# The extra turn in the middle of an expert stream, and three blocks' records written earlier

## The chip, the cores and the metric

The kernel runs on one core of a Trainium2 chip. The metric is the device time of one execution in microseconds (us). The median of three runs of the kernel before is 436.33 us (435.52 to 436.38).

## What is computed

One layer of a graph network, then a mixture of experts, over 1024 nodes with 512 features in float32:

```python
x = x + relu(segment_sum(edge_weight[:, None] * (layernorm(x) @ W)[src], dst) + bias)   # 16384 edges
xt = layernorm(x)
scores = sigmoid(xt @ Wg.T + bg);  w, idx = top_k(scores, 2);  w = w / w.sum(-1)        # 64 experts
nx = standardised rows of xt
h1 = nx @ (gamma[e][:, None] * W1[e]) + ...;  h3 = the same with W3                      # 512 x 256 per expert
y = sum over the two chosen experts e of w[e] * ((silu(h1) * h3) @ W2[e] + b2[e])
x = x + y + (a small shared expert on every row)
```

The reference computes every expert for every row and weights most of them with zero. The kernel only computes the two that a row has chosen. The weights of all 64 experts are read once: 1.5 MB for each expert.

## The kernel before

**First stage (to about 165 us).** The edges are turned into a dense matrix of 1024 x 1024 sums, and the graph layer is eight blocks of 128 rows. For each block s GpSimd computes the deviations of the second norm (`deviations(s)`, L540 to L550), ScalarE writes the standardised rows, SP stores them in DRAM as `nx_rows`, TensorE and VectorE route them, and GpSimd prepares the list (`values`, L558) and the shared expert's rows (`stacked`, L561 to L572). Every engine works in its own order, which is written out by hand, and waits on semaphores for the others.

**Lists.** For every expert there is a list of records (token, destination) in DRAM, `slots`. Records of blocks 0 to 4 (`DRAM_BLOCKS` = 5) are written there with two indirect scatters of 128 records of 8 bytes each (`scatter_records`, L533) while the stage runs. Then SP loads the first 64 places of each list (L380, semaphore `list_in`), and TensorE adds the records of blocks 5 to 7 to it on the chip. DRAM gets these three blocks' records too, since experts with over 64 tokens continue there, and only the overflow uses them. In the kernel before this is done after the first four gathers.

**The stream (from about 170 us).** There are 33 turns. A turn j takes a pair of experts: up to 64 tokens of each are gathered from `nx_rows` by GpSimd (L588), turned by TensorE (L1464), scaled by VectorE, multiplied with W1 and W3 (`up`, L1476), turned (L1498), put through SiLU on ScalarE (L734) and multiplied by the other half on VectorE (L1133). They are then multiplied with W2 (`down`, L1506), copied out by ScalarE (L741) and scattered by GpSimd to `totals` in DRAM (L592). One turn is the extra one: it takes one chunk of up to 128 tokens of an expert whose list has overflowed, with this one expert's weights alone (`over_up` L1483, `over_down` L1490, `over_silu` L748, `over_product` L1143). `EX` is its number, 31, and `LAST` is 32, so that it stands before the last pair. Which expert it is, is known from a small table early in the stream. Its list is loaded by SP in turn 4 (L387, after all records are written) and converted by VectorE (`over_index`) in turn 16.

**Weights.** Six slots hold a turn's weights (`SLOTS` = 6). SP issues the two up loads (1 MB each, L346) of turn j + 6 when turn j's up product is done (`h_ps`), and the down load (1 MB, L349) of turn j + 5 when turn j - 1's down product is done (`y_ps`). For the extra turn they are 0.5 MB each (L392, L396). All go through SP's queue in this order.

**The end.** When all scatters have landed, SP loads `totals` back in eight loads (L436). The last pair isn't scattered: TensorE puts its rows in place with eight matmuls (L1601), ScalarE and VectorE add up, and SP stores eight blocks.

Of the kernel before, what the change touches and what calls it, by code (L numbers as in the profile page):

```python
# [11 lines left out]
NB = N // P  # L12
# [21 lines left out]
PAIRS = EXPERTS // 2  # L34
OVER = 2 * N // CAP
# [3 lines left out]
SLOTS = RING // 2 + 2  # L39
XG, AHEAD = 4, 4  # L40
YS = 4
NOWHERE = 60000.0
EX, LAST = PAIRS - 1, PAIRS
BY_DVE = 1
XS = EX % YS


def pair_of(j):
    return j if j < EX else PAIRS - 1

# [1 line left out]
def moe_gnn(nc, x, src, dst, ew, W, bias, Wg, bg, gamma, beta, W1, b1, W3, b3, W2, b2,  # L54
# [18 lines left out]
    with ctx:  # L73
# [240 lines left out]
        def _(sp):  # L314
# [87 lines left out]
            for j in range(LAST - SLOTS + 1):  # L402
                if j == AHEAD:
                    sp.wait_ge(tokens_ready, 1)
                    for i in range(2):
                        sp.wait_ge(rec_out[i], 32 * NB // 2)
                    load_over(0)
                sp.wait_ge(h_ps, j + 1)
                if j + SLOTS == LAST:
                    sp.wait_ge(y_ps, j)  # L410
                    load_over_down(0)
                if j + SLOTS == EX:
                    load_over_up(0)
                else:
                    load_up(pair_of(j + SLOTS), j % SLOTS)
                if 1 <= j < LAST - SLOTS:
                    sp.wait_ge(y_ps, j)
                    load_down(j + SLOTS - 1, (j - 1) % SLOTS)
            sp.wait_ge(y_ps, LAST - SLOTS + 1)
            load_down(pair_of(LAST), LAST % SLOTS)  # L420
            R2 = sp.value_load(rounds_sb[0:1, 1:2], min_val=1, max_val=OVER)
# [22 lines left out]
        def _(pool):  # L444
# [129 lines left out]
            for s in range(NB):  # L574
                deviations(s)
                if s > DRAM_BLOCKS:
                    values(s - 1)
                if s >= 1:
                    stacked(s - 1)
                if 1 <= s <= DRAM_BLOCKS:  # L580
                    scatter_records(s - 1)
            values(NB - 1)
            pool.wait_ge(at_ps, 2 * NB)
# [11 lines left out]
            pool.wait_ge(list_ready, 1)  # L595
            for j in range(AHEAD):
                gather(TOK[:, j:j + 1], j)
            stacked(NB - 1)
            pool.wait_ge(list_in, 16)
            for s in range(DRAM_BLOCKS, NB):  # L600
                scatter_records(s)
            pool.wait_ge(zero_out, 16)
            for j in range(LAST + 1):
                b = j + AHEAD
                if b <= LAST:
                    if b >= XG:
                        pool.wait_ge(xe_ps, b - XG + 1)
                    if b == EX:
                        pool.wait_ge(over_ready, 1)
                    gather(TOK[:, pair_of(b):pair_of(b) + 1] if b != EX else over_idx[:, 0:1], b % XG)  # L610
                if j == AHEAD:
                    pool.wait_ge(share_out, 16)
                    pool.wait_ge(share_at_ready, 1)
                    g.indirect_dma_start(wsh, None, shares, bass.IndirectOffsetOnAxis(ap=share_at, axis=0),
                                         bounds_check=2 * N - 1, oob_is_err=False).then_inc(wsh_in, 16)
                if j < LAST:
                    pool.wait_ge(y_ready, j + 1)
                    scatter(DST[:, j:j + 1] if j != EX else over_idx[:, 1:2], j % YS)
            pool.wait_ge(tokens_ready, 1)
            R2 = pool.value_load(rounds_sb[0:1, 1:2], min_val=1, max_val=OVER)  # L620
            with pool.If(R2 > 1):
# [11 lines left out]
        def _(act):  # L633
# [117 lines left out]
            for j in range(PAIRS + 1):  # L751
                if j >= 2:
                    act.wait_ge(hT_ps, j - 1)
                if j < LAST:
                    hidden(j, j % 2)
                if j:
                    if j - 1 >= YS:
                        act.wait_ge(y_out[(j - 1) % YS], 16 * ((j - 1) // YS))
                    result(j - 1, (j - 1) % 2, (j - 1) % YS)
                if j == LAST:  # L760
                    hidden(j, j % 2)
                if j >= 2:
                    act.wait_ge(hT_ready, j - 1)
                if j == EX:
                    act.wait_ge(tokens_ready, 1)
                    over_silu(j, j % 2, 0)
                    R2 = act.value_load(rounds_sb[0:1, 1:2], min_val=1, max_val=OVER)
                else:
                    silu(j, j % 2, lambda h: slice(2 * pair_of(j) + h, 2 * pair_of(j) + h + 1))
            act.wait_ge(y_out[LAST % YS], 16 * (LAST // YS))  # L770
            result(LAST, LAST % 2, LAST % YS)
            with act.If(R2 > 1):
# [16 lines left out]
        def _(dve):  # L789
# [367 lines left out]
            for j in range(PAIRS + 1):  # L1157
                if j == 0:
                    over_table()
                if j == 1:  # L1160
                    over_experts()
                    last_shares()
                if j + 1 <= LAST and j + 1 != EX:
                    if j >= 1:
                        dve.wait_ge(h_ps, j)
                    rows(j + 1, (j + 1) % 2)
                if j == 0:
                    for b in range(3, LATE):
                        add_shared(b)
                    dve.wait_ge(stack_ready, NB)  # L1170
                if j == 2:
                    stack_out(NB - 1, bank[5])
                if j in late_turn:
                    add_shared(LATE + late_turn.index(j))
                if j == PAIRS // 2:
                    over_index(0)
                if j + 1 == EX:
                    dve.wait_ge(tokens_ready, 1)
                    at = over_at_expert(0)
                    dve.wait_ge(h_ps, j)  # L1180
                    over_rows(j + 1, (j + 1) % 2, at)
                if j >= 2:
                    dve.wait_ge(y_ps, j - 1)
                if j == EX:
                    over_product(j, j % 2, at)
                    dve.wait_ge(wsh_in, 16)
                    link(v.tensor_copy(tokf, TOK[:, pair_of(LAST):pair_of(LAST) + 1]))
                    link(v.tensor_scalar(token_at, iota[:, 0:NB], -float(P), tokf, ALU.mult, ALU.add))
                    for i in range(NB):
                        ins = v.tensor_scalar(place_last[i], iota[:, :], token_at[:, i:i + 1], wsh, ALU.is_equal, ALU.mult)  # L1190
                    ins.then_inc(last_places, 1)
                else:
                    product(j, j % 2, lambda h: slice(2 * pair_of(j) + h, 2 * pair_of(j) + h + 1))
                if j == EX:
                    R2 = dve.value_load(rounds_sb[0:1, 1:2], min_val=1, max_val=OVER)
            with dve.If(R2 > 1):
                with dve.Fori(1, R2) as t:
# [28 lines left out]
        def _(pe):  # L1226
# [352 lines left out]
            with pe.If(R2 > 1):  # L1579
                with pe.Fori(1, R2) as r:  # L1580
# [2 lines left out]
                    hold(pe)  # L1583
                    turn_rows(0, 0)
                    pe.wait_ge(xe_ready, j + 1)
                    pe.wait_ge(w13_in[OS], r * 32 + (32 * (PAIRS // SLOTS) + 32))
                    hold(pe)
                    over_up(0)
                    turn_hidden(j, 0)
                    whole_bank(bank[0])  # L1590
                    pe.wait_ge(w2_in[OS], r * 16 + (16 * (PAIRS // SLOTS) + 16))
                    pe.wait_ge(y_ready, j)
                    hold(pe)
                    over_down(j, 0)
# [31 lines left out]
```

## Time and profile before

| | us |
|---|---|
| median of three runs | 436.33 |
| the profiled execution | 438.14 |
| its span | 436.4 |
| TensorE busy | 398.3 (91%) |
| VectorE busy | 212.7 (49%) |
| ScalarE busy | 156.8 (36%) |
| GpSimd busy | 172.7 (40%) |

The span is the time from the first to the last instruction of the profiled execution; its own time contains a little more around it. Busy times are sums over the whole span, and stages with different bounds are mixed in them. A wait is shown as the idle time before an instruction with what ended it. A transfer has two numbers: when its instruction was issued, and the time from there to its landing.

### The profile page before, as it was taken

The numbers are of one execution on the slowest core, as the hardware profiler recorded it, in microseconds if no ns is written. First come the engines' busy times: TensorE is split into PE (matmuls) and PEld (weight loads), VectorE is DVE, ScalarE is ACT, GpSimd is POOL, SyncE is SP. The second block draws the span as 40 slices with busy tenths as digits, with TensorE's granted clock in tenths as the row PEclk, the third lists the DMA queues.
The fourth block names the chain that finished last, engine by engine and source line by source line (L and its number), as shares of the span: only waits on it lengthen the run. The fifth ranks groups of instructions, "written<-read, shape, count | busy, mean of one in ns | idle before, by whom it ended". The sixth has DMA issues, their size and how long they took to land.

```text
span 436.4 us, 6405 instructions
## 1 busy us (share of the span) xinstructions
PE 398.3 (91%) x1898; PEld 208.4 (48%) x1899; DVE 212.7 (49%) x696; ACT 156.8 (36%) x387; POOL 172.7 (40%) x275
## 2 busy tenths in 40 slices
PE   6988999999999998999999999978978877988986
PEld 5556768655655556434344344433333333443431
DVE  8899998136566676542332332331223213112437
ACT  8777786223233220423233233321231231132232
POOL 2769996315655646632432232231122123111100
PEclk9999999999999998999999999998999999898999
DMA  7999970400004572789999999999999999999378
GB/s 239 222 341 410 404 273 32 141 25 26 24 24 159 207 293 74 199 324 407 403 407 407 408 403 409 407 407 408 408 403 408 408 406 405 405 401 379 152 258 324
DMA packets 44022, 129.15 MB, mean 296 GB/s; under 512 B 8054, under 2 KB 9270, under 8 KB 43858
## 3 DMA queue, kind: packets, MB, share of 16 engines
q1 hardware_dynamic: 38242, 120.45, 73.1%
q0 software_dynamic: 5744, 8.28, 5.3%
q8 instruction: 16, 0.26, 0.2%
q14 instruction: 20, 0.16, 0.1%
HBM read 119.64 MB, written 17.85 MB: 315 GB/s over the span
## 4 chain that ended last, share of the span: by engine, by line
PE 71%; issue 8%; POOL 6%; DMA 6%; DVE 5%; SPq 1%; ACT 1%; DVEq 0%; ACTq 0%; POOLq 0%
PE bank L1476 24%; PE bank L1339 13%; PE bank L1506 11%; PE bank L1498 4%; PE bank L1288 4%; PE bank L1464 3%; PE bank L1261 3%; DMA A<-nx_rows,A 2%; DMA w<-totals 2%; PE bank L1327 2%; PE bank L1360 1%; POOL slots L533 1%; POOL M L500 1%; POOL AT L500 1%; PE bank L1348 1%
## 5 line engine op out<-in xcount | busy, mean ns | idle before, releaser
L1133 DVE SCALAR_TENSOR_TENSOR osl<-bank,b13T,osl 128x64 f32<-128x64 f32 x128 | 27.5, 277 | 162.0 <-ACT osl L734 162.0
L1476 PE MATMUL bank<-w,xhT 128*64 128x512 f32 x352 | 85.7, 630 | 15.0 <-issue 14.3
L727 ACT COPY xh<-bank 128x512 f32<-128x512 f32 x33 | 19.3, 585 | 145.1 <-PE bank L1476 142.1
L1339 PE MATMUL bank<-HW,AT 128*128 128x512 f32 x128 | 58.2, 593 | 0.0
L1476 PEld LDWEIGHTS bank<-w,xhT 128*64 128x64 f32 x352 | 26.4, 143 | 59.0 <-issue 56.8
L592 POOL DMA_INDIRECT totals<-GW,A x16 | 16.0, 1003 | 89.5 <-PE bank L1464 70.5
L592 POOL DMA_INDIRECT totals<-osl,A x16 | 16.1, 1004 | 71.2 <-PE bank L1464 61.8
L1506 PE MATMUL bank<-w,osl 128*64 128x512 f32 x176 | 41.9, 594 | 0.5 <-DVE osl L1133 0.5
L588 POOL DMA_INDIRECT A<-nx_rows,A x33 | 34.1, 1032 | 12.3 <-issue 9.8
L1339 PEld LDWEIGHTS bank<-HW,AT 128*128 128x128 f32 x128 | 22.9, 191 | 21.0 <-issue 21.0
L643 ACT ACTIVATE osl<-iota,eT 128x128 f32<-128x128 f32 x90 | 27.8, 387 | 9.9 <-PE bank L1288 9.9
L734 ACT ACTIVATE osl<-bank,b13T 128x64 f32<-128x64 f32 x128 | 29.8, 314 | 3.8 <-PE bank L1498 0.9
L1498 PEld LDWEIGHTS bank<-ident,xh 128*128 128x128 f32 x132 | 18.3, 208 | 26.8 <-issue 25.1
L1261 PE MATMUL bank<-GW,xhT 128*128 128x512 f32 x64 | 29.3, 597 | 1.0 <-DMA GW<-in_L_gnn_W_dram 1.0
L500 POOL TENSOR_SCALAR AT<-iota,small 128x128 f32<-128x128 f32 x30 | 25.5, 861 | 1.5 <-POOL small L489 1.4
L1498 PE MATMUL bank<-ident,xh 128*128 128x128 f32 x132 | 24.6, 309 | 0.7 <-ACT xh L727 0.7
L1506 PEld LDWEIGHTS bank<-w,osl 128*64 128x64 f32 x176 | 13.3, 137 | 25.0 <-issue 24.8
L1464 PE MATMUL bank<-ident,A 128*128 128x128 f32 x132 | 21.6, 286 | 1.0 <-DMA A<-nx_rows,A 1.0
L1476 PE MATMUL bank<-HW,xhT 128*64 128x512 f32 x80 | 18.3, 597 | 4.3 <-issue 4.3
L1118 DVE TENSOR_TENSOR xhT<-xhT,bT 128x512 f32<-128x512 f32 x31 | 21.4, 692 | 1.1
L1117 DVE TENSOR_TENSOR xhT<-bank,gT 128x512 f32<-128x512 f32 x31 | 21.1, 680 | 0.3 <-PE bank L1464 0.3
L500 POOL TENSOR_SCALAR M<-iota,small 128x128 f32<-128x128 f32 x23 | 19.7, 865 | 2.4 <-POOL small L489 1.5
(238 smaller groups left out, 594.9 us busy)
## 6 DMA issues: line engine op xcount, KB each, us to landing
w<-in_L_ffn_W_dram SPq DMA_DIRECT2D x66, 1024.0 KB, 19.0
A<-in_L_ffn_W_dram SPq DMA_DIRECT2D x15, 1024.0 KB, 18.6
HW<-in_L_ffn_W_dram SPq DMA_DIRECT2D x10, 1024.0 KB, 19.2
AT<-in_L_ffn_W_dram SPq DMA_DIRECT2D x5, 1024.0 KB, 19.9
totals<-w SPq DMA_DIRECT2D x1, 4096.0 KB, 26.4
w<-totals SPq DMA_DIRECT2D x8, 512.0 KB, 7.5
out_dram<-X SPq DMA_DIRECT2D x8, 256.0 KB, 2.3
X<-in_x_dram SPq DMA_DIRECT2D x3, 512.0 KB, 8.6
```

The source lines that it names most:

```text
L500: ins = g.tensor_scalar(Mq[q % 4][:, k, :], iota[:, :], keyw[h % 2][:, 0, t:t + 1], keyw[h % 2][:, 1, t:t + 1], ALU.is_equal, ALU.mult)
L588: g.indirect_dma_start(xg[b], None, nx_rows, bass.IndirectOffsetOnAxis(ap=index, axis=0), bounds_check=N - 1, oob_is_err=False).then_inc(x ...
L592: g.indirect_dma_start(totals, bass.IndirectOffsetOnAxis(ap=index, axis=0), ysb[b], None, bounds_check=2 * N - 1, oob_is_err=False).then_i ...
L643: ins = a.activation(osl[:, h % 2, k, :], iota[:, :], ACT.Abs, bias=eT[:, 1, ds(j * 32 + 8 * h + k, 1)])
L734: ins = a.activation(sl[b][:, m, CAP * h:CAP * h + CAP], bank[4][:, m * P + CAP * h:m * P + CAP * h + CAP], ACT.Silu, bias=b13T[:, 0, m, c ...
L1133: ins = v.scalar_tensor_tensor(hT[b][:, m, CAP * h:CAP * h + CAP], bank[4][:, (HC + m) * P + CAP * h:(HC + m) * P + CAP * h + CAP], b13T[: ...
L1261: ins = t.matmul(bank[6 + u][:, :], xhT[:, u, c, :], GW[:, c, :], start=(c == 0), stop=(c == DC - 1))
L1339: ins = t.matmul(bank[4 + s % 2][:, :], AT[:, s % 2, k, :], HW[:, k, :], start=(k == 0), stop=(k == NB - 1))
L1464: ins = t.transpose(bank[b][:, c * P:(c + 1) * P], xg[i][:, c:c + DC * (P - 1) + 1:DC], ident[:, :])
L1476: ins = t.matmul(bank[2 + b][CAP * h:CAP * h + CAP, :], xe[b][:, c, CAP * h:CAP * h + CAP], up_w[v][:, h, :, c, :], start=(c == 0), stop=( ...
L1498: ins = t.transpose(bank[4][:, i * P:(i + 1) * P], hraw[b][:, at:at + HC * (P - 1) + 1:HC], ident[:, :])
L1506: ins = t.matmul(bank[6 + b][CAP * h:CAP * h + CAP, :], hT[b][:, m, CAP * h:CAP * h + CAP], down_w[v][:, h, m, :], start=(m == 0), stop=(m ...
```

## The change

Two things are changed. `EX` becomes 17, so that the extra turn stands in the middle, turns 18 to 32 take pairs 17 to 31, and all loads, lists and registers of the extra turn follow it. Its list is converted in turn 8. And each of the last three blocks' records are written in GpSimd's loop like those of the others. The first of them waits for the list's load (`list_in`) in this place, and block 7's are written after the first four gathers and before `stacked(7)`.

```diff
--- before.py
+++ after.py
@@ -40,13 +40,13 @@
 XG, AHEAD = 4, 4
 YS = 4
 NOWHERE = 60000.0
-EX, LAST = PAIRS - 1, PAIRS
+EX, LAST = PAIRS // 2 + 1, PAIRS
 BY_DVE = 1
 XS = EX % YS
 
 
 def pair_of(j):
-    return j if j < EX else PAIRS - 1
+    return j if j < EX else j - 1
 
 
 
@@ -406,16 +406,18 @@
                         sp.wait_ge(rec_out[i], 32 * NB // 2)
                     load_over(0)
                 sp.wait_ge(h_ps, j + 1)
-                if j + SLOTS == LAST:
-                    sp.wait_ge(y_ps, j)
-                    load_over_down(0)
                 if j + SLOTS == EX:
                     load_over_up(0)
-                else:
+                elif j + SLOTS < LAST:
                     load_up(pair_of(j + SLOTS), j % SLOTS)
-                if 1 <= j < LAST - SLOTS:
+                if j >= 1:
                     sp.wait_ge(y_ps, j)
-                    load_down(j + SLOTS - 1, (j - 1) % SLOTS)
+                    if j + SLOTS - 1 == EX:
+                        load_over_down(0)
+                    else:
+                        load_down(pair_of(j + SLOTS - 1), (j - 1) % SLOTS)
+                if j + SLOTS == LAST:
+                    load_up(pair_of(LAST), LAST % SLOTS)
             sp.wait_ge(y_ps, LAST - SLOTS + 1)
             load_down(pair_of(LAST), LAST % SLOTS)
             R2 = sp.value_load(rounds_sb[0:1, 1:2], min_val=1, max_val=OVER)
@@ -577,7 +579,9 @@
                     values(s - 1)
                 if s >= 1:
                     stacked(s - 1)
-                if 1 <= s <= DRAM_BLOCKS:
+                if s >= 1:
+                    if s - 1 == DRAM_BLOCKS:
+                        pool.wait_ge(list_in, 16)
                     scatter_records(s - 1)
             values(NB - 1)
             pool.wait_ge(at_ps, 2 * NB)
@@ -595,10 +599,8 @@
             pool.wait_ge(list_ready, 1)
             for j in range(AHEAD):
                 gather(TOK[:, j:j + 1], j)
+            scatter_records(NB - 1)
             stacked(NB - 1)
-            pool.wait_ge(list_in, 16)
-            for s in range(DRAM_BLOCKS, NB):
-                scatter_records(s)
             pool.wait_ge(zero_out, 16)
             for j in range(LAST + 1):
                 b = j + AHEAD
@@ -615,7 +617,7 @@
                                          bounds_check=2 * N - 1, oob_is_err=False).then_inc(wsh_in, 16)
                 if j < LAST:
                     pool.wait_ge(y_ready, j + 1)
-                    scatter(DST[:, j:j + 1] if j != EX else over_idx[:, 1:2], j % YS)
+                    scatter(DST[:, pair_of(j):pair_of(j) + 1] if j != EX else over_idx[:, 1:2], j % YS)
             pool.wait_ge(tokens_ready, 1)
             R2 = pool.value_load(rounds_sb[0:1, 1:2], min_val=1, max_val=OVER)
             with pool.If(R2 > 1):
@@ -764,9 +766,10 @@
                 if j == EX:
                     act.wait_ge(tokens_ready, 1)
                     over_silu(j, j % 2, 0)
-                    R2 = act.value_load(rounds_sb[0:1, 1:2], min_val=1, max_val=OVER)
                 else:
                     silu(j, j % 2, lambda h: slice(2 * pair_of(j) + h, 2 * pair_of(j) + h + 1))
+                if j == LAST - 1:
+                    R2 = act.value_load(rounds_sb[0:1, 1:2], min_val=1, max_val=OVER)
             act.wait_ge(y_out[LAST % YS], 16 * (LAST // YS))
             result(LAST, LAST % 2, LAST % YS)
             with act.If(R2 > 1):
@@ -1172,7 +1175,7 @@
                     stack_out(NB - 1, bank[5])
                 if j in late_turn:
                     add_shared(LATE + late_turn.index(j))
-                if j == PAIRS // 2:
+                if j == 2 * AHEAD:
                     over_index(0)
                 if j + 1 == EX:
                     dve.wait_ge(tokens_ready, 1)
@@ -1183,15 +1186,15 @@
                     dve.wait_ge(y_ps, j - 1)
                 if j == EX:
                     over_product(j, j % 2, at)
+                else:
+                    product(j, j % 2, lambda h: slice(2 * pair_of(j) + h, 2 * pair_of(j) + h + 1))
+                if j == LAST - 1:
                     dve.wait_ge(wsh_in, 16)
                     link(v.tensor_copy(tokf, TOK[:, pair_of(LAST):pair_of(LAST) + 1]))
                     link(v.tensor_scalar(token_at, iota[:, 0:NB], -float(P), tokf, ALU.mult, ALU.add))
                     for i in range(NB):
                         ins = v.tensor_scalar(place_last[i], iota[:, :], token_at[:, i:i + 1], wsh, ALU.is_equal, ALU.mult)
                     ins.then_inc(last_places, 1)
-                else:
-                    product(j, j % 2, lambda h: slice(2 * pair_of(j) + h, 2 * pair_of(j) + h + 1))
-                if j == EX:
                     R2 = dve.value_load(rounds_sb[0:1, 1:2], min_val=1, max_val=OVER)
             with dve.If(R2 > 1):
                 with dve.Fori(1, R2) as t:
@@ -1583,12 +1586,12 @@
                     hold(pe)
                     turn_rows(0, 0)
                     pe.wait_ge(xe_ready, j + 1)
-                    pe.wait_ge(w13_in[OS], r * 32 + (32 * (PAIRS // SLOTS) + 32))
+                    pe.wait_ge(w13_in[OS], r * 32 + 32 * ((LAST - OS) // SLOTS + 1))
                     hold(pe)
                     over_up(0)
                     turn_hidden(j, 0)
                     whole_bank(bank[0])
-                    pe.wait_ge(w2_in[OS], r * 16 + (16 * (PAIRS // SLOTS) + 16))
+                    pe.wait_ge(w2_in[OS], r * 16 + 16 * ((LAST - OS) // SLOTS + 1))
                     pe.wait_ge(y_ready, j)
                     hold(pe)
                     over_down(j, 0)
```

## Rows read from the trace of the kernel before

**Rows 1.** The page: granted clock and transfers in 40 slices of 10.9 us.
```profile
PEclk9999999999999998999999999998999999898999
...
GB/s 239 222 341 410 404 273 32 141 25 26 24 24 159 207 293 74 199 324 407 403 407 407 408 403 409 407 407 408 408 403 408 408 406 405 405 401 379 152 258 324
```

**Rows 2.** Chain of waits, 277 to 292 us: start us, us, what.
```profile
277.49 3.58 PE bank L1476 x16
...
283.95 0.66 issue
...
291.13 2.06 issue
```

**Rows 3.** Chain of waits, 352 to 400 us.
```profile
352.88 3.65 PE bank L1476 x16
...
392.86 1.74 issue
394.60 5.35 PE bank L1476 x16
```

**Rows 4.** Timeline, all engines, 402 to 417 us: start, duration, instruction, idle before.
```profile
402.44 0.93 ACT L734 ACTIVATE osl<-bank,b13T 128x64 f32<-128x64 f32 x4
402.66 3.60 PE L1483 MATMUL bank<-w,xhT 128*128 128x512 f32 x8
...
408.98 0.62 ACT L748 ACTIVATE osl<-bank,b13T 128x128 f32<-128x128 f32 x2 [0.16 <-PE bank L1498]
...
414.02 0.98 POOL L592 DMA_INDIRECT totals<-osl,A x1 [3.45 <-ACT osl L741]
414.19 3.65 PE L1476 MATMUL bank<-w,xhT 128*64 128x512 f32 x16
416.64 4.25 SPq L436 DMA_DIRECT2D w<-totals  x8
```

**Rows 5.** Timeline of SP's queue, 150 to 189 us and at 390 us.
```profile
150.82 0.69 SPq L380 DMA_DIRECT2D A<-slots  x1
...
177.47 5.90 SPq L346 DMA_DIRECT2D w<-in_L_ffn_W_dram  x4
184.20 0.37 SPq L349 DMA_DIRECT2D w<-in_L_ffn_W_dram  x1
188.95 0.88 SPq L346 DMA_DIRECT2D w<-in_L_ffn_W_dram  x2
...
390.36 2.41 SPq L346 DMA_DIRECT2D w<-in_L_ffn_W_dram  x1
```

**Rows 6.** Transfers, 391 to 392 us: count, size, us from issue to landing.
```profile
w<-in_L_ffn_W_dram SPq DMA_DIRECT2D x1, 1024.0 KB, 18.9
```

**Rows 7.** Busy time by stretch; the last column is GB/s.
```profile
185.00:188.00 3.00, 3.00 (x17) 1.17 (x18) 2.13 (x6) 0.80 (x4) 2.05 (x2) 1.00 0.65 60
```

**Rows 8.** Timeline of GpSimd, 156 to 183 us.
```profile
156.56 0.19 POOL L545 TENSOR_SCALAR small<-small 128x1 f32<-128x1 f32 x1 [3.58 <-DVE small L988]
...
164.31 0.61 POOL L558 TENSOR_TENSOR eT<-GW,stats 128x256 f32<-128x256 f32 x1 [2.83 <-DVE GW L1014]
...
182.53 1.06 POOL L588 DMA_INDIRECT A<-nx_rows,A  x1 [0.30 <-issue]
```

**Rows 9.** The scatter of turn 30 (L592), issued at 409.6.
```profile
DMA to landing us min/median/max: 3.0/3.0/3.0
```

**Rows 10.** L380 (list load); L533 from 100 to 150; L533 from 170 on.
```profile
DMA to landing us min/median/max: 2.2/2.2/2.2
...
DMA to landing us min/median/max: 2.2/2.5/5.2
...
L533 POOL DMA_INDIRECT slots<-small,GW x6: 954/958/1072, 174.8 to 181.3; - x6
...
DMA to landing us min/median/max: 2.1/5.9/6.0
```

**Rows 11.** Timeline of VectorE, 180 us.
```profile
180.41 0.86 DVE L1133 SCALAR_TENSOR_TENSOR osl<-bank,b13T,osl 128x64 f32<-128x64 f32 x4 [2.20 <-ACT osl L734]
```


## The prediction

> Turns are called T0 to T32 below. In the kernel before, T31 is the extra turn (one expert, half the weights) and T32 works on the last pair; after the change the extra turn is T17 and T18 to T32 work on pairs 17 to 31.
>
> **What bounds the kernel now.** First the page's 40 slices [rows 1]. The row GB/s stands near 405 from slice 18 (about 196 us) to slice 35 (about 393 us). Before and after that it is uneven. So half of the span is one stream of weights. The chain of waits then tells who follows whom. T16 starts at 277.49 and TensorE is ready for T17 at 283.95, 6.46 us later, as in the turns before it, with no wait. From T17 on there is a wait before each turn, 0.66 us at first and 2.06 us before T18 [rows 2]. From T25 to T30 the starts lie (394.60 - 352.88) / 5 = 8.34 us apart, with 1.74 us of waiting before T30 [rows 3]. TensorE needs 6.46 and the stream 8.34. The last third is bound by the transfers, and what counts is the moment from which they run without a gap, and the bytes.
>
> Then the end, in the timeline of all engines [rows 4]. T31 starts at 402.66, T32 at 414.19, the scatter of T31 is issued at 414.02, and at 416.64 the queue of SP sends the loads of the totals, which waited for that scatter. The second half of T32's up weights landed at 390.36 + 18.9 = 409.3 [rows 5, 6]. T32 started 4.9 us after its data. So from T30's start on, TensorE's own chain of work sets the end, and the stream sets when T30 starts.
>
> Last, the beginning of the stream. From 185 to 188 us the transfers fall to 60 GB/s [rows 7], although SP had issued five megabytes from 177.47 to 184.20 [rows 5]. Against 410 this loses 3 x (410 - 60) / 410 = 2.6 us. All that is late here is late at the end.
>
> **The extra turn in the middle.** Work on the engines is moved, not removed. Its bytes are not changed either: 1.57 MB less at T17 and 1.57 MB more at T31, at 406 GB/s 3.9 us each. What changes is who waits. At T17 TensorE now waits 0.66 us; after the change T17's weights are half and T18's arrive 3.9 us earlier, 289.3 instead of 293.19, while TensorE is ready at about 283.95 + 6.46 = 290.4. So T18 waits for nothing and T19 is again bound by data. From there each turn up to T30 starts 3.9 us earlier: T30 at 390.7.
>
> T31 is now a full pair. Its data come one period later, 390.7 + 8.34 = 399.0; TensorE is ready at 390.7 + 6.46 = 397.2. It starts at 399.0 where the extra turn started at 402.66. The extra turn's matmuls took 3.60 us [rows 4] and a pair's 3.65 (T32) [rows 4]: the same. ScalarE's part is 0.93 for a pair and 0.62 for the extra turn, 0.31 more [rows 4]. I take as much again for VectorE, an estimate by the same ratio of four instructions to two. T32's start follows T31's by 414.19 - 402.66 = 11.53, now 12.15: 411.1. Its weights keep their place, last in the queue, and land at 409.3, so they are no bound, with 1.8 us to spare. If this cover goes, T32 starts at 409.3 plus whatever the stream is late.
>
> The profiled execution had one more thing: T30's matmuls took 5.35 us instead of 3.65, at half the clock (1.2 instead of 2.4 GHz), after the wait of 1.74 us [rows 1, 3]. That is 1.70 us in the chain of the end. With it, T32 moves from 414.19 to 411.1, 3.1 us; without it the start before would have been 412.5, and the gain is 1.4. In the row of the granted clock three of slices 27 to 36 hold such a fall, in some fourteen turns that wait, so the usual execution has none at T30. The execution profiled took 438.14 and the median is 436.33, 1.81 less. One such fall would account for it, though it proves nothing. I take 1.4 against the median, and keep 3.1 as the other end.
>
> Of that something is lost. The last scatter ahead of the totals carried an overflow list; now it carries a pair. The one of T30, issued at 409.6, landed in 3.0 us [rows 9]; the one of T31 let SP go on after 416.64 - 414.02 = 2.6 [rows 4]: 0.4 lost. Sum of this part: 1.0 us, at most 2.7.
>
> The rest of it costs nothing. The overflow list is asked for at T4 and converted at T8 instead of T16. A load that enters the full stream lands in some 19 us [rows 6]; from T4 to T8 it is 4 x 6.46 = 25.8. The weights' addresses are read on SP while 19 us of transfers are queued. VectorE's copy and its tables for the last pair stay in the turn before T32.
>
> **The records.** Six indirect scatters, (181.3 - 174.8) / 5 = 1.3 us apart, are issued between the fourth and the fifth gather [rows 10], and the fifth gather follows at 182.53 [rows 8]. Four of them move into the loop. For block 5, GpSimd has idled 3.58 us when its next work comes at 156.56 [rows 8]; it was free at 152.98. The list load is issued at 150.82 and lands 2.2 later, 153.0 [rows 5, 10]. Two scatters take 2.6, so they end at 155.6, 0.9 before block 7's deviations, for which all wait. For block 6 the gap before 164.31 is 2.83 [rows 8], and 2.6 just fit. Block 7's two scatters now precede its stacking, which ends at about 177.4 instead of 174.8. VectorE asks for it when it has added two shared blocks, at 180.41 - 2.20 = 178.2, and then idles until 180.41 for ScalarE [rows 11]: 0.8 to spare, and 3.0 before anything moves. The fifth gather is issued at about 177.5 instead of 182.53. Turns that no longer wait for it would start earlier, but what is late next is T17's data, so that this is worth nothing at the end.
>
> The gain, if any, is in the stream. At least half of the six scatters landed only after 5.9 to 6.0 us, where most scatters between 100 and 150 us took 2.2 to 2.5 [rows 10]. The hole of rows 7 opens as the last of them goes through, and no other such hole is on the page. After the change only block 7's two scatters stand before the first weights at 177.47 [rows 5], and none among them. No row prices a stream without them. The bounds are 0 and 2.6 us. I take 2.6, because the coincidence is the only thing that sets this place apart from the stream that follows, in which gathers and scatters of whole rows also run and cost no hole. The cover for it is there: five megabytes are 12.8 us of transfer from 178.5 at the earliest, so until 191, and SP issues the next at 188.95 [rows 5].
>
> The Trainium skill (DMA: Bandwidth & Descriptors, Back-pressure in remote DMA) says that stalled writes stall the other queues of their transfer engine too, though of transfers between cores; the same page's Specifications say that writes under 512 bytes are read and written back. By that rule the hole goes. The landings of rows 10 agree with it, and no run here yet shows its cause.
>
> **The sum.** 436.33 - 1.0 - 2.6 = 432.7. Against the profiled execution it would be 438.14 - 2.7 - 2.6 = 432.8 if T30's slow clock is absorbed there.
>
> **The rivals.**
> A. The hole stays, or comes back elsewhere in the first microseconds of the stream, because it belongs to a stream's start and not to the records. The place is the stream's first ten microseconds as well as the last scatters', and no row parts the two. Then only the extra turn counts: 436.33 - 1.0 = 435.3.
> B. The clock. T31 is now a full turn that waits 1.8 us right before the end, where it didn't wait. If the clock is granted at 1.2 GHz there, T31 takes 1.70 more: 434.4 with the hole gone, 437.0 with it. Three falls in fourteen waits speak for a smaller chance. [...]
> C. Slower. GpSimd works in order, and the new wait for the list stands ahead of block 7's deviations; ScalarE, TensorE, the routing, the list, the gathers and so the whole stream wait for these. It decides when the list lands after 154.0, a microsecond later than now. With a landing of 5.2 us, the slowest scatter between 100 and 150 us [rows 10], it is 156.0, the scatters end at 158.5, and all is 2.0 us later. With the hole in place: 436.33 - 1.0 + 2.0 = 437.3. Against it: before the change the same load took 2.2 [rows 10], and nothing is put ahead of it.
> D. The change does nothing at the end, because T31's up weights come later than 399.0: every microsecond of it is one lost, and at 400.5 the extra turn's gain is gone. This is within A's spread.
>
> **How the numbers follow.** Forecast (hole gone) 0.45, 432.7; A and D 0.33, 435.3; B 0.12, 434.4 or 437.0; C 0.10, 437.3. The range of 8 in 10 reaches from the forecast with the larger gain of the extra turn, 431.0, a little lower for the unknown, to 436.3, which takes in A and half of B. A change of 0.2% (0.87 us) is about what can be measured here, so faster means under 435.5 and slower over 437.2. Faster: 0.45 + 0.18 of A + 0.07 of B = 0.70. Same: the rest of A and B, 0.20. Slower: 0.10.
>
> **What would show it.** In the profile after: no stretch under 300 GB/s between 180 and 190; the fifth gather near 177.5 and landed before TensorE asks; T18 without a wait, T19 to T30 about 6.5 us earlier than now (3.9 and 2.6); a wait of about 1.8 before T31; the totals' loads issued near 411.3 without the hole, near 413.9 with it. Wrong would be: block 7's deviations later than 156.6, a hole that has only moved, T31 over 1.5 us later than its place in this sum.

## The result, and the profile after

The kernel after takes 431.48 us (median of 4 runs, 430.81 to 432.00) beside 436.35 for the kernel before in the same comparison (4 runs, 435.52 to 436.38): a ratio of 0.989 with an interval of 0.9865 to 0.9915, or 4.9 us less. The profiled execution took 432.0, with a span of 430.2, where it was 438.14 and 436.4.

The page of the kernel after, granted clock and transfers in 40 slices of 10.8 us (compare [rows 1]):

```profile
PEclk9999999999999998999999999999989998899999
...
GB/s 254 211 335 408 406 287 47 137 31 26 25 25 63 281 232 146 151 402 410 400 407 405 410 406 407 406 407 406 405 406 409 405 408 404 406 399 406 231 273 325
```

Slice 17 (counted from 0), the first full one of the stream, now moves 402 GB/s. It was 324. The hole of [rows 7] is filled, as the busy time by stretch shows (last column GB/s, the one before it the share of time in which the transfer engines had packets in work, 1.03 in the full stream):

```profile
182.00:185.00 3.00, 3.00 (x18) 1.05 (x13) 2.13 (x9) 0.94 (x2) 0.00 (x0) 1.00 1.03 417
185.00:188.00 3.00, 3.00 (x19) 1.45 (x19) 1.69 (x6) 1.16 (x5) 1.67 (x2) 1.00 1.04 412
188.00:191.00 3.00, 3.00 (x17) 0.82 (x13) 0.74 (x2) 0.59 (x1) 0.41 (x1) 1.00 0.97 373
```

GpSimd's timeline in the kernel after answers to [rows 8] and [rows 10]. L535 are the scatters of records, L547 begins block 7's deviations, L560 stands for its values, and L592 are the gathers:

```profile
154.04 1.11 POOL L535 DMA_INDIRECT slots<-small,GW  x1 [0.81 <-DMA A<-slots]
155.46 1.17 POOL L535 DMA_INDIRECT slots<-small,GW  x1 [0.30 <-issue]
156.82 0.19 POOL L547 TENSOR_SCALAR small<-small 128x1 f32<-128x1 f32 x1 [0.20 <-DVE small L991]
...
163.46 0.96 POOL L535 DMA_INDIRECT slots<-small,GW  x1 [0.30 <-issue]
164.63 0.61 POOL L560 TENSOR_TENSOR eT<-GW,stats 128x256 f32<-128x256 f32 x1 [0.21 <-issue]
...
177.56 1.33 POOL L592 DMA_INDIRECT A<-nx_rows,A  x1 [0.26 <-issue]
```

Block 5's two scatters wait 0.81 us for the list and end at 156.63. Block 7's deviations, which still wait for VectorE, come at 156.82, 0.2 us behind them. The fifth gather is issued at 177.56.

The chain of waits around the extra turn in its new place (L1486), in the kernel after (compare [rows 2]):

```profile
276.63 3.58 PE bank L1479 x16
...
283.09 3.44 PE bank L1486 x8
...
289.55 3.58 PE bank L1479 x16
...
296.00 3.58 PE bank L1479 x16
...
303.32 3.58 PE bank L1479 x16
...
309.78 2.62 issue
312.40 5.35 PE bank L1479 x16
```

T16 to T20 follow each other without a wait (ahead of T20 stand 0.86 us of the shared expert's products, L1412). TensorE is bound by data again only at T21. The same chain at the end, T30 and T31 (compare [rows 3]):

```profile
386.25 1.78 issue
388.03 3.65 PE bank L1479 x16
...
394.56 1.44 issue
396.00 3.65 PE bank L1479 x16
```

And the timeline of all engines at the end (compare [rows 4]): T31's down product waits for VectorE, its scatter is issued at 407.60, and the totals' loads at 410.63.

```profile
404.19 1.94 PE L1509 MATMUL bank<-w,osl 128*64 128x512 f32 x8 [1.04 <-DVE osl L1136]
...
407.60 0.98 POOL L596 DMA_INDIRECT totals<-osl,A  x1 [3.79 <-ACT osl L743]
407.97 3.65 PE L1479 MATMUL bank<-w,xhT 128*64 128x512 f32 x16
...
410.63 3.96 SPq L438 DMA_DIRECT2D w<-totals  x8
```

T30 starts 6.57 us earlier than before (394.60 - 388.03), and the totals' loads 6.01 earlier (416.64 - 410.63). Between the two lie 22.60 us, where they were 22.04.

### The profile page after: what moved, and what is told of

Same layout as the page of the kernel before. It is cut to its first block, busy times and chain, and to the rows that moved or that the text cites. A ratio compares the mean times of both kernels' runs of the same rounds, so it can differ in the third digit from the quotient of the medians.

```text
span 430.2 us, 6405 instructions
## 1 busy us (share of the span) xinstructions
PE 398.4 (93%) x1898; PEld 207.4 (48%) x1899; DVE 213.2 (50%) x696; ACT 156.9 (36%) x387; POOL 174.1 (40%) x275
## 4 chain that ended last, share of the span: by engine, by line
PE 80%; issue 6%; DVE 5%; POOL 4%; DMA 3%; ACT 1%; SPq 1%; DVEq 0%; POOLq 0%; ACTq 0%
PE bank L1479 27%; PE bank L1342 13%; PE bank L1509 12%; PE bank L1501 5%; PE bank L1291 4%; PE bank L1467 4%; PE bank L1264 3%; DMA w<-totals 2%; PE bank L1236 2%; PE bank L1330 2%; PE bank L1363 2%; POOL M L502 1%; POOL AT L502 1%; PE bank L1351 1%; PE bank L1412 1%
## 5 line engine op out<-in xcount | busy, mean ns | idle before, releaser
L1479 PE MATMUL bank<-w,xhT 128*64 128x512 f32 x368 | 87.6, 618 | 11.5 <-issue 11.5
L1509 PE MATMUL bank<-w,osl 128*64 128x512 f32 x184 | 43.7, 593 | 1.6 <-DVE osl L1136 1.6
L592 POOL DMA_INDIRECT A<-nx_rows,A x33 | 34.3, 1039 | 12.3 <-issue 9.7
L1479 PE MATMUL bank<-A,xhT 128*64 128x512 f32 x80 | 20.0, 645 | 1.9 <-issue 1.9
```

What stands on the lines that cost most here:

```text
L592: g.indirect_dma_start(xg[b], None, nx_rows, bass.IndirectOffsetOnAxis(ap=index, axis=0), bounds_check=N - 1, oob_is_err=False).then_inc(x ...
L1479: ins = t.matmul(bank[2 + b][CAP * h:CAP * h + CAP, :], xe[b][:, c, CAP * h:CAP * h + CAP], up_w[v][:, h, :, c, :], start=(c == 0), stop=( ...
L1509: ins = t.matmul(bank[6 + b][CAP * h:CAP * h + CAP, :], hT[b][:, m, CAP * h:CAP * h + CAP], down_w[v][:, h, m, :], start=(m == 0), stop=(m ...
```

## The experiments

The kernel before was run again beside each group of experiments: 436.98 us beside e1 to e4, 436.13 beside e5 to e8 and 436.24 beside e9 to e12 (medians of 14, 22 and 17 runs). Each experiment's ratio is against its own group's.

**The two halves, e1_extra_only and e2_records_only.** e1 is the kernel after with GpSimd's part as before:

```diff
-                if s >= 1:
-                    if s - 1 == DRAM_BLOCKS:
-                        pool.wait_ge(list_in, 16)
+                if 1 <= s <= DRAM_BLOCKS:
                     scatter_records(s - 1)
...
-            scatter_records(NB - 1)
             stacked(NB - 1)
+            pool.wait_ge(list_in, 16)
+            for s in range(DRAM_BLOCKS, NB):
+                scatter_records(s)
```

> Only the extra turn is moved (turn 17 instead of 31); the records of blocks 5 to 7 stay between the fourth and the fifth gather. Theory S (the four record scatters among the first weights open the hole of 2.6 us): the hole at 185 to 188 us is still there, under 150 GB/s, and the time is 436.35 - 1.0 to - 2.3 = 434.0 to 435.4. Rival G (the hole belongs to the fifth gather being issued late, beside the second turn's loads): the same here. Rival P (the hole was a chance of one execution and the records are worth nothing): the whole gain of 4.9 us is here, 431.5, and no hole. In the chain of waits under all three: turns 19 to 30 start 3.9 us earlier than before, turn 31 waits for its weights.

e2 is the other half: the records as after, the extra turn as before.

```diff
-EX, LAST = PAIRS // 2 + 1, PAIRS
+EX, LAST = PAIRS - 1, PAIRS
```

> Only the records are written earlier; the extra turn stays turn 31. Theory S: no stretch under 300 GB/s between 182 and 188 us, turn 30 starts 2.6 us earlier than 394.6, and the time is 436.35 - 2.6 = 433.8. Rival G: the same here, since the fifth gather too is issued near 177.5. Rival P: 436.3, no difference. Rival C of the prediction (the wait for the list holds GpSimd up): over 436.9, with block 7's deviations later than 157.5.

e1 took 434.32 us (0.9939, interval 0.9916 to 0.9962), 2.7 less than before. e2 took 433.33 (0.9911, 0.988 to 0.9941), 3.7 less. Each half is a gain, and the two add up to the whole or somewhat more (6.3 beside 4.9 and, in e10 below, 5.3), within the intervals. T30 starts at 389.51 in e1, 5.09 earlier than before and not 3.9, since the hole was smaller, and at 392.39 in e2, 2.21 earlier. The stretch from 185 to 188 us, first in e1, then in e2:

```profile
185.00:188.00 3.00, 3.00 (x18) 1.34 (x18) 1.84 (x6) 1.01 (x5) 1.82 (x2) 1.00 1.00 199
```

```profile
185.00:188.00 3.00, 3.00 (x20) 1.74 (x20) 1.29 (x5) 1.52 (x5) 1.23 (x2) 1.00 1.04 406
```

The hole is there where the six scatters stand together and gone where they don't. It is smaller in e1 than in [rows 7], 1.5 us by the same working, and its 199 GB/s are above the 150 that were expected at most.

**The kernel before once more, e3_before_again.** No edit: is [rows 7] one execution's accident, and is T30's slow clock?

> The kernel before, unchanged, for a second profile. Theory S and rival G: the hole between 184 and 189 us is there again, under 150 GB/s for about 3 us. Rival P: it is elsewhere or missing. On the clock: if the fall at turn 30 is tied to the wait there, turn 30's up matmuls take 5.35 us again; if it is by chance, 3.65, and the span is about 1.7 us under 436.4.

One execution, 436.21 us. The same stretch, and the chain at T30:

```profile
185.00:188.00 3.00, 3.00 (x16) 0.86 (x12) 2.15 (x6) 0.10 (x1) 1.94 (x2) 1.00 0.58 137
```

```profile
393.43 5.35 PE bank L1476 x16
```

Both are back. So the hole belongs to the kernel, though its size varies, and T30's 5.35 us are no accident either: e2, whose end is that of the kernel before, has them too (its profile is of the slowest of its seven runs, 436.86).

```profile
392.39 5.35 PE bank L1476 x16
```

**Is it the late gather? e4_filler.** The six scatters also held up the fifth gather. Here six vector operations without use stand in their place, in the kernel after:

```diff
             stacked(NB - 1)
+            for i in range(6):
+                link(g.tensor_scalar(M[:, 0, 0, :], iota[:, :], 1.0, 0.5, ALU.mult, ALU.mult))
             pool.wait_ge(zero_out, 16)
```

> The changed kernel, with six chained GpSimd operations of about 0.9 us each on an unused buffer put between block 7's stacking and the fifth gather. The fifth gather is so issued near 183, as in the kernel before, but no scatter stands in its place. Theory S: no hole, 431.5 as the changed kernel, and at most turn 3 waits a microsecond for the gather's rows, worth nothing at the end. Rival G: the hole is back, 431.5 + 2.6 = 434.1.

431.24 us (0.9867, 0.9834 to 0.99). The fifth gather is issued at 180.57, 3.0 later than in the kernel after and 2.0 earlier than in the kernel before, and there is no hole:

```profile
185.00:188.00 3.00, 3.00 (x17) 1.23 (x17) 1.95 (x6) 0.93 (x4) 1.93 (x2) 1.00 1.04 412
```

A gather that comes 3.0 us late makes no hole. The next run has the gather early and the scatters behind it.

**Scatters among the first weights, the gather early, e5_scatters_after_gather.** The scatters of blocks 5 and 6 are taken out of the loop and come right behind the fifth gather:

```diff
+                if j == 0:
+                    pool.wait_ge(list_in, 16)
+                    for s in range(DRAM_BLOCKS, NB - 1):
+                        scatter_records(s)
```

> The changed kernel, but the four record scatters of blocks 5 and 6 are issued right after the fifth gather, at about 179 to 184 us: the fifth gather is early and the scatters stand among the first weights. Theory S (the scatters open the hole): transfers under 250 GB/s somewhere between 184 and 189, and about 1.5 to 2.6 us more than the changed kernel (against this call's runs of before, a ratio near 0.994 instead of 0.989). Rival G (only the late fifth gather matters): no hole, ratio 0.989 or lower.

432.85 us (0.9922, 0.9896 to 0.9947), between after and before, and 1.2 over e6 of its group (below). The gather is issued at 178.43, the four scatters from 179.85 to 183.72. From 182 to 185 the stream still runs at 414, and then:

```profile
185.00:188.00 3.00, 3.00 (x18) 1.67 (x18) 1.17 (x5) 1.52 (x5) 1.12 (x2) 1.00 1.08 248
188.00:191.00 3.00, 3.00 (x15) 0.93 (x13) 1.27 (x3) 0.59 (x1) 0.93 (x1) 1.00 0.93 290
```

Against the kernel after's 412 and 373 this loses 3 x ((412 - 248) + (373 - 290)) / 410 = 1.8 us: four scatters among the first weights make a hole like that of e1's six, though the gather is early. So the late gather is not the cause. The share of 1.08 beside 248 GB/s says that the transfer engines had packets in work all this time. They moved little, but were not idle here. In the kernel before it is otherwise: there the share in the hole is 0.65 [rows 7], after 1.36 just ahead of it:

```profile
182.00:185.00 3.00, 3.00 (x19) 1.34 (x14) 1.76 (x5) 1.30 (x3) 1.28 (x2) 1.00 1.36 405
```

**Does it belong to the start of the stream? e7_scatters_t8, e11_eight_scatters, e12_small_reads.** e7 is the kernel after, with the four scatters once more in the middle of the running stream (the records are written twice). e11 does the same with eight (blocks 3 to 6), and e12 reads as many places of the same list as e7 writes, with four indirect gathers into a buffer that nobody uses:

```diff
+                if j == 8:
+                    pool.wait_ge(over_in, 16)
+                    for i in range(2):
+                        pool.wait_ge(rec_out[i], 32 * NB // 2)
+                    for s in (5, 6):
+                        scatter_records(s)
```

> The changed kernel with the same four record scatters (blocks 5 and 6, the same values to the same places) issued a second time in turn 8, in the middle of the full stream. Theory S1 (four small scatters stop any stream): a hole of 1.5 to 2.6 us near 226 us and that much more time, ratio near 0.994. Theory S2 (they hurt only while the stream starts): no slice under 380 GB/s there, and at most 0.3 us more than the changed kernel.

> The changed kernel with eight record scatters (blocks 3 to 6, the same values to the same places) issued a second time in turn 8. Four of them made a hole of 1.2 us near 242 us. Theory N (the price goes by the number of small writes): a hole or holes of 2.4 us in all, and 2 us over the changed kernel. Theory O (the price is for one event, however many writes): 1.2 us again.

> The changed kernel with four indirect gathers of records (128 of 8 bytes each, from the same list in DRAM into an unused buffer) in turn 8, where the other two kernels have scatters. Theory W (it is the small writes to DRAM that stop the stream): no stretch under 350 GB/s, the time of the changed kernel within 0.3 us. Rival R (any burst of small transfers from GpSimd's queue does it): a hole of about 1.2 us as with four scatters.

The stretch in which the writes go through, in e7:

```profile
242.00:244.00 2.00, 1.22 (x10) 0.74 (x7) 0.00 (x0) 1.07 (x2) 0.00 (x0) 1.00 1.07 197
244.00:246.00 2.00, 2.00 (x13) 0.93 (x13) 0.86 (x5) 0.93 (x4) 1.28 (x2) 1.00 0.96 379
```

In e11:

```profile
242.00:244.00 2.00, 0.89 (x6) 0.01 (x1) 0.00 (x0) 0.00 (x0) 1.70 (x2) 1.00 1.03 355
244.00:246.00 2.00, 0.00 (x0) 0.00 (x0) 0.00 (x0) 0.10 (x1) 1.39 (x3) 1.00 1.21 246
246.00:248.00 2.00, 1.37 (x10) 1.24 (x12) 0.00 (x0) 0.49 (x1) 0.73 (x1) 1.00 0.81 179
...
250.00:252.00 2.00, 2.00 (x8) 0.58 (x6) 1.63 (x6) 0.23 (x2) 1.51 (x2) 0.58 1.03 257
```

In e12:

```profile
242.00:244.00 2.00, 1.06 (x9) 0.92 (x8) 0.00 (x0) 1.15 (x3) 0.00 (x0) 1.00 1.01 403
```

So the hole can be moved into the steady stream: four scatters cost ((406 - 197) + (406 - 379)) x 2 / 406 = 1.2 us of it, and eight cost 3.1 over the six stretches from 242 to 254 by the same sum. The four reads cost nothing there. TensorE's own idle time in these rows is another thing: it waits for ScalarE's copy of the hidden rows, which comes late in all three, and what holds the copy isn't shown. It is there in e12 too, 0.9 us, without a hole. Timed, e7 took 431.99 us (0.9906, 0.9879 to 0.9933), e11 434.18 (0.9948, 0.9922 to 0.9974) and e12 431.33 (0.9863, 0.9825 to 0.9901). Against the kernel after in the same group (e10, 430.9) that is 3.3 more for e11 and 0.4 for e12, within noise. e7 is 0.35 above e6 of its group, which is too little to be sure of. For e7 a hole of 1.5 to 2.6 us and as much more time had been expected, so its times alone don't show the price. e11's do: more than twice the hole of four, where 2.4 us had been expected for a price by number. TensorE idles for 3.7 us in e11's rows, but T30 starts at 390.93, 2.90 after that of the kernel after, and the missing bytes alone make 2.9 (3.1, less 0.2 for 361 instead of 354 GB/s from 178 to 191).

**The place of the extra turn, e6_extra_29.** Does the gain come from the middle, or only from no longer being next to the last?

```diff
-EX, LAST = PAIRS // 2 + 1, PAIRS
+EX, LAST = PAIRS - 3, PAIRS
```

> The changed kernel with the extra turn as turn 29 instead of 17. Theory M (what pays is that a half turn of weights leaves the end, so that turns 30 and 31 start earlier and turn 31 works under its wait): the same as the changed kernel within 0.7 us, turn 30 near 388.0, turn 31 near 396.0. Rival X (it pays only where TensorE is the bound up to turn 17 and the half load fills the crossing): about 2.7 us slower than the changed kernel. On the clock: if the slow clock at turn 30 comes with a turn 31 that is the extra one, turn 30's matmuls take 3.65 here.

431.64 us (0.9889, 0.9863 to 0.9915), the same as the kernel after. The profile is of the slowest of its seven runs, 434.81: its stream began late (the first load is issued at 180.54 instead of 177.91), so T30 starts at 392.25 and T31 at 398.70 where 388.0 and 396.0 were expected. The chain at T28, the extra turn T29, and T30:

```profile
377.56 5.35 PE bank L1479 x16
...
385.79 3.44 PE bank L1486 x8
...
392.25 3.58 PE bank L1479 x16
```

With the extra turn at 29, T30 has no wait before it, and in this trace, with T28 at the slow clock, neither has T31. What pays is that half a turn's weights no longer stand right before the end; at 29 or at 17 made no difference in the times.

**The price of the slow clock, e8_before_filled.** The kernel before, with twelve transposes without use on TensorE in each of turns 27 to 30, so that it isn't idle before T30:

```diff
+                if j == 27:
+                    pe.wait_ge(z_added, NB)
+                if 27 <= j <= 30:
+                    keep_busy(bank[5], 12)
```

> The kernel before, with twelve 128x128 transposes of the identity on TensorE in each of turns 27 to 30, ahead of the wait for the weights (about 1.4 us each, in the place of a wait of 1.8). It prices the slow clock at turn 30 by itself. Theory K (the clock falls to 1.2 GHz at turn 30 in the kernel before in nearly every execution, and the changed kernel gains 1.7 us by not having it there): turn 30's matmuls take 3.65 us, and the time is 1.3 to 1.7 us under before, ratio 0.996 to 0.997. Rival L (it falls there by chance, seldom outside the profiles): no difference in the median, ratio 1.000, or slower by up to 0.5 us for the filling.

```profile
395.25 3.65 PE bank L1476 x16
```

T30 runs at full clock, and from its start to the totals' loads (415.52) the profile has 20.27 us, where the three with the slow clock have 22.04, 22.05 and 21.85. But timed it took 436.54 (1.0012, 0.9991 to 1.0032): no gain. Its own profile had the largest hole of all:

```profile
185.00:188.00 3.00, 2.41 (x14) 1.52 (x16) 0.70 (x4) 1.86 (x6) 1.01 (x1) 1.00 0.64 37
```

That goes with a T30 that starts 0.65 us late in this one execution, but doesn't explain the missing gain over 12 runs.

**A better version? e9_hidden_first, beside e10_after_again.** In the kernel after TensorE waits 1.04 us for VectorE in T31. e9 puts T31's turning of the hidden rows ahead of T30's down product, on TensorE (shown) and ScalarE, to fill it:

```diff
-                if 1 <= j < LAST:
+                if 1 <= j < LAST - 1:
                     down_of(j - 1)
+                if 1 <= j < LAST:
                     pe.wait_ge(hT_ready, j)
                 turn_hidden(j, j % 2)
+                if j == LAST - 1:
+                    down_of(j - 1)
```

> The changed kernel, where in turn 31 alone TensorE turns the hidden rows before it multiplies turn 30's down weights, and ScalarE computes turn 31's SiLU before it copies turn 30's result. In the changed kernel TensorE idles 1.0 us for turn 31's product while nothing is left to do (404.19, idle before 1.04); with the down product put there, turn 31's own down product ends about 0.9 us earlier. Theory M (from turn 31's start on, the chain of work sets the end): 0.6 to 0.9 us less than the changed kernel in the profile, ratio to it 0.998. Rival (the weights of turn 32 or the totals' loads are the bound): the same as the changed kernel.

> The changed kernel, unchanged, to stand beside the others on this chip and for a second profile: ratio to before 0.989, no stretch under 300 GB/s between 182 and 188 us, turn 30 and turn 31 at full clock if that is a habit of the kernel and not chance.

e9 took 432.05 us (0.9879, 0.9837 to 0.9921), e10, the kernel after unchanged, 430.9 (0.9865, 0.9827 to 0.9903). First e9's chain at T30 and T31, then e10's:

```profile
387.18 5.35 PE bank L1482 x16
...
395.40 3.61 PE bank L1482 x16
```

```profile
386.89 3.65 PE bank L1479 x16
...
394.90 3.65 PE bank L1479 x16
```

In e9 the scatter of T31 is issued at 406.99 and in e10 at 406.49, both 11.59 us after T31's start, where 0.6 to 0.9 less had been expected. TensorE's wait for VectorE is gone, but it now waits 0.83 us for ScalarE's copy of T31's hidden rows. No version beat the kernel after.

## Why the prediction was right, point by point

The forecast was 432.7 with the hole gone, and 431.48 was measured. Its mechanism was the right one, the hole gone with the scatters and half a turn less to wait for ahead of the end. Together its two terms were 1.2 us too small.

**What bounds the kernel.** Right. The start of T30 follows the bytes that the first microseconds of the stream have moved. From 178 to 191 us, in the kernel before and after:

```profile
178.00:191.00 13.00, 13.00 (x65) 5.01 (x63) 5.89 (x23) 4.95 (x13) 6.42 (x7) 1.00 0.96 268
```

```profile
178.00:191.00 13.00, 13.00 (x66) 5.43 (x65) 6.79 (x24) 5.40 (x13) 2.97 (x3) 1.00 0.92 354
```

That is (354 - 268) x 13 / 406 = 2.75 us. T30 is 6.57 us earlier, and with the 3.9 of half a turn's weights the two make 6.65. Among kernels with their extra turn in one place the rule holds as closely: before and e2 (268 and 338 in this stretch) should be 2.24 apart at T30 and are 394.60 - 392.39 = 2.21; e1 and after (304 and 354) should be 1.60 apart and are 1.48. The loosest pair is e5 and after: 2.37 by the rule and 1.90 in the traces.

The bytes of this stretch hold two things, the hole and the moment at which the stream begins, and the second differs between executions (177.47 before, 177.91 after, 176.56 in e10). Counted from the first load's issue the two come apart:

| from the first load's issue to T30's start | us |
|---|---|
| extra turn at 17, no scatters in the stream (after, e4, e9, e10, e12) | 210.12, 209.94, 210.00, 210.33, 210.38 |
| extra turn at 17, with scatters (e7 and e5 four, e1 six, e11 eight) | 211.14, 211.47, 211.75, 213.31 |
| extra turn at 31, no scatters (e2) | 214.05 |
| extra turn at 31, six scatters (e3, before, e8) | 216.66, 217.13, 217.70 |

So half a turn's weights are 3.9 (214.05 less the 210.15 of the first row's mean), and the scatters cost between 1.0 (e7) and 3.7 (e8), 3.1 in the profile of the kernel before. The change as a whole is 7.0 by this count, and 0.4 of it is hidden in the 6.57 because the stream after began later.

**The extra turn.** The steps up to T30 held. T18 doesn't wait, and half a turn's weights gave the 3.9 (table above). The trace after has no wait until T21, where the forecast had T19 bound by data. This came from the stream's own gain of 2.75 and costs nothing. T31 waits 1.44 (1.8 was forecast) and starts at 396.0 (396.4 with the hole's 2.6 taken off 399.0). The step that was mis-sized is the way from T30 to the totals' loads: the term of 1.0 us, which is 1.4 at T32 (3.1 where T30's clock was slow before) less 0.4 at the last scatter. The runs show these sizes:

| from T30's start to the totals' loads | us |
|---|---|
| extra turn at 31, T30 at half clock (before, e2, e3) | 22.04, 22.05, 21.85 |
| extra turn at 31, T30 at full clock (e8, with filler) | 20.27 |
| extra turn at 17 (after, e1, e4, e5, e7, e10, e11, e12) | 22.60, 22.38, 22.21, 22.78, 22.23, 22.60, 22.26, 22.24 |

The mean of the last row is 22.4. So the gain is 3.9 - (22.4 - 20.3) = 1.8 where T30 had the full clock before, and 3.9 - (22.4 - 22.0) = 3.5 where it ran at half of it; I had 1.0 and 2.7. These 0.8 lie in T30 to T31 (7.97 in the kernel after, taken as 8.34), T31 to T32 (11.97, taken as 12.15) and the last scatter (2.6 to 3.2 to SP in these eight, 2.8 in the mean, taken as 3.0). Which of the two cases is the usual one, I argued from three falls in fourteen waits, and the profiles speak against it: with the extra turn at 31 and no filler T30 is slow in 3 of 3, with the extra turn at 17 in the order of the kernel after in 0 of 8 (after, e1, e4, e5, e7, e10, e11, e12). Timed alone, the part gave 2.7 (e1), with an interval of about 1.7 to 3.7. That lies midway and excludes neither end. The same part with the records already moved is e2 against e4 of its group, 433.33 - 431.24 = 2.1. This and that e8's filler gave nothing speak for the smaller end. This contradiction stays open: which of the two executions is typical can't be read from so few profiles, and why the filler's gain in the trace isn't found in the times is not known.

**The records.** Right, and right about the cause that the forecast rested on, a coincidence of 60 GB/s with the last scatters. e1, e3 and e8 have the hole, with 1.5 to 2.7 us lost from 185 to 188, and e2, e4, e10 and after don't have it. e5 puts 1.8 us of it back, and e7 moves a smaller one to 57 us later. Timed alone, the part gave 3.7 (e2), and e4, which has both changes and no hole, is 3.1 under e1 of its group. Both are more than the 2.6 I took, and so is the 3.1 of the table above: the scatters also took from the stream ahead of the stretch from 185 to 188 (374 GB/s from 182 to 185 in e3), and the size of the hole differs between executions. The fifth gather's issue was forecast at 177.5 and came at 177.56. That it is worth nothing at the end also held: e4 delays it by 3.0 us without loss.

The Trainium skill's rules that the prediction weighed (DMA: Bandwidth & Descriptors, Back-pressure in remote DMA and Specifications) gave the right sign. e5's and e11's transfer shares of 1.08 and 1.21 beside 248 and 246 GB/s agree with stalled writes that hold other queues' packets, here inside one core. The 0.65 in the hole of the kernel before (0.58 in e3, 0.64 in e8) doesn't follow from it by itself: for a third of those 3 us, in the mean, an engine had no packet in work. No run isolates the read and write back of small writes.

**Rival A** (the hole stays or belongs to the stream's start) fell with after, e2 and e7. **Rival B** (T31 at half clock) didn't come: T31's matmuls took 3.65 us after a wait of 1.44 in after, and 3.65 in the seven others of that order too. T28 in the kernel after (5.35 us from 371.37, after a wait of 1.93) shows that the clock does fall in other turns of this kind. **Rival C** (the wait for the list) was nearer than I priced it. I gave it 0.9 us of room, and the trace has at most 0.2. The list's load was issued at 151.08 and landed in 2.3, so at 153.4, but the first scatter was issued only at 154.04, 0.6 after it, a step that I had priced at nothing; a pair then took 2.59. Block 7's deviations came at 156.82, which is later than the 156.6 that I had called a sign of being wrong. But they came 5.74 us after the list's load was issued, as before (156.56 - 150.82), so they were late because the load was, and nothing was lost in this execution. The 0.2 is no more than the step between two instructions of GpSimd (0.21 ahead of block 7's values below), so a list that lands later would probably move everything behind it. Block 6's scatters leave as little: block 7's values now wait 0.21 for nothing but GpSimd's own order. **Rival D** had no case: T31's weights came in their place.

## What to carry to other kernels

A load stream that sets the pace is best priced by its bytes in its first microseconds. Three microseconds of it at 60 instead of 410 GB/s are paid in full 200 us later, and no engine's busy time shows it. It helps to count from the stream's first load, since its beginning differs between executions. Many small indirect writes belong where no such stream runs, even if the engine that issues them has time among the loads. And half a turn's load saved ahead of the last wait for data is a gain of that load's time, less what the full turn then costs at the end. Whether it is moved 2 or 14 turns ahead made no difference here.

## What the hardware showed that was not expected

Four indirect scatters of 128 records of 8 bytes, 4 KB in all, take 1.2 us from a stream of 406 GB/s (e7), eight take 3.1 (e11), while four small indirect reads leave 403 (e12). While the stream falls the transfer engines can show as busy (1.07 at 197 GB/s in e7, 1.21 at 246 in e11) or as partly idle (0.65 at 60 in the kernel before, 0.81 at 179 in e11). Scatters of whole rows (128 of 2 KB each) go on in every turn and leave the stream at 406. Where the weights are held up, and whether it is the size of the records that matters, isn't shown.
